# Decoder layer on one core: another split of the row-maximum pieces between the first stage and the attention loop

## The reference, cut to what matters

```
scores = jnp.einsum('bhqd,bhkd->bhqk', q, k) / jnp.sqrt(jnp.float32(Dh))
causal = jnp.tril(jnp.ones((S, S), dtype=bool))
scores = jnp.where(causal[None, None], scores, jnp.float32(-jnp.inf))
attn = jax.nn.softmax(scores, axis=-1)
out = jnp.einsum('bhqk,bhkd->bhqd', attn, v)
```

## Time and profile before

| | |
|---|---|
| median of 3 runs | 839.01 us |
| profiled execution, its own time | 840.59 us |
| its span, first to last instruction | 838.9 us |
| granted TensorE clock, mean | 0.984 |
| first stage, up to the first scores | 0 to 87.99 us |
| attention, heads 0 to 15 | 87.99 to about 470.3 us |
| one head of the steady state | 23.75 us |
| PE busy in such a head | 23.40 us |
| DVE busy in such a head | 22.41 us |
| ACT busy in such a head | 19.00 us |

### The profile page before, as it was taken

One profiled execution on the slowest core, in us unless ns is written; L12 is line 12 of the kernel. 1 busy time (PEld: TensorE's weight loads), 2 busy tenths in 40 slices (PEclk: granted clock), 3 DMA queues, 4 the chain that ended last, 5 costly groups with the idle time before them and its releaser, 6 DMA issues. The chain is left out here.

```text
span 838.9 us, 19596 instructions
## 1 busy us (share of the span) xinstructions
PE 783.6 (93%) x7434; PEld 496.9 (59%) x7435; DVE 559.2 (67%) x1072; ACT 512.3 (61%) x756; POOL 303.8 (36%) x226
## 2 busy tenths in 40 slices
PE   5899899999999999999998797889999999999994
PEld 1367344444443444444433585778888888877883
DVE  4575699999999999999980496973333333222395
ACT  4441687778887877788879487254444444343543
POOL 5040595555333355554550112132333333301121
PEclk9999799999999999999999999999999999999998
DMA  8783343334444443334232598452222222221362
GB/s 295 131 214 152 113 152 108 103 123 133 143 151 152 152 132 109 105 133 139 106 115 114 209 398 214 150 190 65 77 75 75 75 75 75 76 58 52 102 195 76
DMA packets 68362, 111.47 MB, mean 133 GB/s; under 512 B 39485, under 2 KB 49918, under 8 KB 63934
## 3 DMA queue, kind: packets, MB, share of 16 engines
q1 hardware_dynamic: 63134, 93.36, 35.7%
q0 software_dynamic: 4816, 16.65, 6.0%
q10 hardware_dynamic: 336, 0.40, 0.4%
HBM read 66.60 MB, written 32.37 MB: 118 GB/s over the span
## 5 line engine op out<-in xcount | busy, mean ns | idle before, releaser
L172 DVE TENSOR_REDUCE partial<-ring 128x1 f32<-128x512 f32 (+3 forms) x510 | 312.8, 670 | 24.2 <-PE ring L154 18.8
L709 ACT ACTIVATE probs<-scores 128x1024 f32<-128x1024 f32 (+1 forms) x320 | 270.5, 902 | 69.6 <-PE scores L747 36.9
L1284 ACT ACTIVATE hid<-turned 128x512 f32<-128x512 f32 (+1 forms) x112 | 65.6, 586 | 160.7 <-PE turned L1445 130.9
L154 PE MATMUL ring<-kstack,qstack 48*128 48x512 f16 (+1 forms) x581 | 156.4, 354 | 2.4 <-DVE partial L172 0.2
L774 PE MATMUL acc<-probs,values 128*32 128x512 f32 (+2 forms) x1472 | 156.6, 496 | 0.5 <-ACT acc_sb L714 0.3
L1470 PE MATMUL ops<-weights,work 128*128 (+1 forms) x1320 | 148.9, 273 | 2.7 <-DVE work L1685 1.4
L1445 PE MATMUL turned<-mats,weights 128*128 128x256 f16 (+1 forms) x1344 | 143.6, 262 | 3.2 <-DMA mats<-attn 2.2
L747 PE MATMUL scores<-qstack,kstack 49*128 49x512 f16 (+3 forms) x640 | 135.1, 352 | 7.2 <-ACT probs L709 5.9
L1685 DVE TENSOR_TENSOR work<-hid,work 128x512 f16<-128x512 f32 (+1 forms) x112 | 76.8, 690 | 94.9 <-ACT work L1289 94.8
L1470 PEld LDWEIGHTS ops<-weights,work 128*128 128x128 f16 x1320 | 128.4, 98 | 18.9 <-issue 3.8
L684 POOL TENSOR_TENSOR a_w_in<-a_w_in,w_scale 128x2304 f32<-128x2304 f32 x16 | 64.4, 4027 | 202.6 <-DMA a_w_in<-w_all 202.6
(11 more groups left out here) (203 smaller groups left out, 742.5 us busy)
## 6 DMA issues: line engine op xcount, KB each, us to landing
a_w_in<-w_all SPq DMA_DIRECT2D x16, 1152.0 KB, 9.1
w_split_d<-a_w_out SPq DMA_DIRECT2D x16, 1152.0 KB, 5.7
weights<-w_split_d SPq DMA_DIRECT2D x6, 2048.0 KB, 19.8
weights<-w_split_d POOLq DMA_DIRECT2D x3, 2048.0 KB, 12.1
qstack<-q_split SPq DMA_DIRECT2D x72, 64.0 KB, 2.7
kstack<-k_split SPq DMA_DIRECT2D x72, 64.0 KB, 2.8
weights<-by_token SPq DMA_DIRECT2D x8, 512.0 KB, 7.6
attn<-xT SPq DMA_DIRECT2D x4, 512.0 KB, 7.4
```

The source lines that it names most:

```text
L154: mm = nc.tensor.matmul(bank[:, at:at + w], qstack[rows, slot, t * P:(t + 1) * P], kstack[rows, slot, c:c + w], start=True, stop=not diagonal)
L172: return nc.vector.tensor_reduce(out=found[:, places[0]:places[-1] + 1:step], in_=bank[:, 0:WIDTH[n]].rearrange("p (k w) -> p k w", k=len( ...
L709: nc.scalar.activation(probs[:, quad % NPROBS, at:at + w], scores[half][:, first:first + w], ACT.Exp, scale=QK_SCALE).then_inc(exp_done, 1)
L1284: nc.scalar.activation(h32, hps[b].rearrange("p (j n) -> p j n", n=TW)[:, :, 0:w], ACT.Silu, scale=1.0 / WSCALE).then_inc(silu_done, 1)
```

## The change

It changes how many pieces stand where. No matmul and no reduction is added or dropped over the whole kernel.

- The first stage forms all 35 pieces of head 0 and all of head 1 (70 in place of 50). `pieces_behind` puts a pair behind every t step and behind every second m step but the last.
- The 490 pieces that are left, of heads 2 to 15, form one sequence, each head's in the order of the string `ORDER`. `deal_ring` fills the places of heads 0 to 14 with it: 34 in each of heads 0 to 2, 33 in each of heads 3 to 13, 25 in head 14.
- The places of a head hold 33 pieces: quad 1 has one in place of two behind its weighing, and quad 8 loses the one behind its first half. Kinds are no longer tied to quads; a head's q piece drifts from quad 1 (head 0) to quad 9 (head 13).
- The turned maximum M of a head stands wherever 4 pieces have passed since its last piece. It drifts with the sequence: M1 at the very start, M3 in quad 2 of head 2, M7 in quad 4 of head 6, M13 in quad 8 of head 12. M14 stands behind the weighing of quad 8 of head 13. M15 stands at quad 8 of head 14, right after the last piece.
- PE waits for a stack at the first piece of each head. `neg_max` of head 1 is reduced at the start of `attend`.

```
-EARLY_QUADS = tuple(range(6, NQUAD))
+ORDER = "wdwwnwqwdnwwwwpwdwwwnwwwwdwwwwwpwnw"
-PLACES = (("", "wd", "w"), ("w", "w", "nw"), ("", "ww", "w"), ("d", "w", "w"), ("", "ww", "Fwp"),
+PLACES = (("", "xx", "x"), ("x", "x", "x"), ("", "xx", "x"), ("x", "x", "x"), ("", "xx", "Fxx"),
...
+FIRST_HEADS = 2
+BEHIND = 4
...
+def deal_ring():
+    left = [("piece", g, n) for g in range(FIRST_HEADS, H) for n in ORDERED]
+    rows = [(g, 0) for g in range(1, FIRST_HEADS)]
...
+                if rows and (passed >= rows[0][1] + BEHIND or not left or rows[0][1] == 0):
+                    entries.append(("max", rows.pop(0)[0], 0))
+                for x in place + ("x" if (s, i) == (1, 2) and h < more else ""):
+                    if x in OTHERS and h > 0:
+                        entries.append((OTHERS[x], h - 1, 0))
+                    if x == "x" and left:
+                        entries.append(left.pop(0))
+                        passed += 1
+                        if not left or left[0][1] != entries[-1][1]:
+                            rows.append((entries[-1][1], passed))
...
-FIRST_PIECES = [*range(NPIECE), *EARLY_PIECES]
+FIRST_PIECES = FIRST_HEADS * [*range(NPIECE)]
...
     if kind == "m":
-        return 2 if n % 4 == 3 else 0
-    return 2 * {"qk": n >= NQ * 4 - 2, "v": n % 2, "t": n % 3 != 2}[kind]
+        return 2 if n % 2 == 1 and n < DC * CT - 1 else 0
+    return 2 * {"qk": n >= NQ * 4 - 2, "v": n % 2, "t": 1}[kind]
...
+                        if e == FIRST_PIECE[g]:
+                            pe.wait_ge(stack_in[g % NSTACK], (g // NSTACK + 1) * STACK_DMAS)
...
+            find_max(1)
```

More of the change, by code:

```diff
@@ L108, in deal_pieces @@
         left.setdefault(kind_of(n), []).append(n)
-    dealt = [[[x if x in OTHERS else left[x].pop(0) for x in place] for place in places] for places in PLACES]
-    assert not any(left.values())
-    return dealt
-DEALT = deal_pieces()
-EARLY_PIECES = [x for s in EARLY_QUADS for place in DEALT[s] for x in place if x not in OTHERS]
-def ring_of(h):
-    def entry(s, x):
-        kind, ahead = OTHERS[x] if x in OTHERS else ("piece", 2 if s in EARLY_QUADS else 1)
-        return (kind, h + ahead, 0 if x in OTHERS else x)
-    return [[[y for y in (entry(s, x) for x in place) if 0 <= y[1] < H] for place in places] for s, places in enumerate(DEALT)]
-RING = [ring_of(h) for h in range(H)]
+    return [left[x].pop(0) for x in ORDER]
+ORDERED = order_pieces()
+def deal_ring():
+    left = [("piece", g, n) for g in range(FIRST_HEADS, H) for n in ORDERED]
+    rows = [(g, 0) for g in range(1, FIRST_HEADS)]
+    more = len(left) - (H - 1) * len("".join(x for places in PLACES for place in places for x in place if x == "x"))
+    more += sum(x == "x" for places in PLACES[NQUAD - 2:] for place in places for x in place)
+    dealt, passed = [], 0
+    for h in range(H):
+        dealt.append([])
+        for s, places in enumerate(PLACES):
+            dealt[h].append([])
+            for i, place in enumerate(places):
+                entries = []
+                if rows and (passed >= rows[0][1] + BEHIND or not left or rows[0][1] == 0):
[8 more added lines that the diff above has]
+                            rows.append((entries[-1][1], passed))
+                dealt[h][s].append(entries)
+    assert not left and not rows
+    return dealt
+RING = deal_ring()
 RING_END = [("fold", H - 1, 0), ("turn", H - 1, 0)]
@@ L132 @@
 FOLDS = [sum(x[0] == "fold" for x in ENTRIES[0:e + 1]) for e in range(len(ENTRIES))]
-LAST_PIECE = {g: e for e, (kind, g, _) in enumerate(ENTRIES) if kind == "piece"}
+FIRST_PIECE, LAST_PIECE = {}, {}
+for e, (kind, g, _) in enumerate(ENTRIES):
+    if kind == "piece":
+        FIRST_PIECE.setdefault(g, e)
+        LAST_PIECE[g] = e
 VFIRST = NT - 5
-FIRST_PIECES = [*range(NPIECE), *EARLY_PIECES]
+FIRST_PIECES = FIRST_HEADS * [*range(NPIECE)]
 def group_rows(group, rows):
@@ L816, in _ @@
                 for s in range(NQUAD):
-                    ahead = h + (2 if s in EARLY_QUADS else 1)
-                    if ahead < H and s in (0, EARLY_QUADS[0]):
-                        pe.wait_ge(stack_in[ahead % NSTACK], (ahead // NSTACK + 1) * STACK_DMAS)
                     for half in range(2):
```

13 lines of the change are left out of this document (7 added, 6 removed).

## The result

The kernel after takes 847.38 us, the median of 4 runs (846.15 to 849.92), where the kernel before took 838.94 beside it (4 runs, 837.18 to 839.31). The ratio is 1.0109, 95% interval 1.0081 to 1.0136: slower by 1.1%, where 836.1 us and a range up to 841.5 were forecast. The profiled execution took 846.15 us, with a span of 844.4.

The account below looks back on a forecast made before the run. PE bounds the first stage; in the loop ACT and PE pace part A (quads 2 to 6), PE and DVE part B (quads 7 to 9, 0, 1). 5.5 - 10.2 + 1.8 = -2.9 us, so 836.1 us, range 831 to 841.5.

Parts of the forecast that it names:

- First stage, +5.5: End of the first stage: ten added pairs at 0.51 us of PE, plus 0.4 for hiding matmuls, cost 5.5 us.
- Rival 3: First stage: DVE falls behind, so the ten pairs cost about 8.5 us, not 5.5; 839 us; chance 0.12.
- End of the loop, +1.8: Head 14 and loop end: fuller quads 6 and 7 0.3, M15's wait 1.1, M14's later row 0.4; 1.8 us.
- rival 4: Seam into the loop: different work spacing spares PE's slow 1.2 GHz stretch, winning 3 us; 833 us; chance 0.12.
- Heads 1 to 13, -9.9 forecast: Attention loop: heads 1 to 5 win 1.05 us each, 6 to 9 0.6, 10 to 13 0.55.
- Quad 8 loses the q piece: Quad 8 and part B: removing q, M and two late bank waits gives 1.27 us, 1.1 after M's new cost.
- In quads 2 to 4 PE has waits for ACT to hide it: Attention loop: q's extra 0.45 us over a w piece is hidden in quads 2 to 4, not in 5 and 6.
- M costs 0.12 to 0.25 where it goes: Attention loop: the moved turned maximum costs 0.12 to 0.25 us in its new quad.
- The second piece behind quad 1: nothing is won there: Quad 1: the removed piece ran beside the first on PE, winning nothing; DVE saves 0.61 us part A doesn't need.
- Rival 2: Loop's PE queue: work only moves, a head wins 0.3 us; 842.1 us; decides below 0.52 a head; chance 0.20.
- Rival 1: Attention loop: DVE alone paces the heads, each piece less worth 0.614 us in all 14 heads; 830.9 us; chance 0.10.
- The prediction's own sign of being wrong: Wrong if heads' gain doesn't depend on where q stands, or the first stage's end moves over 7 us.

Follow-up runs that it names:

- Half reductions: Kernels before and after, each reduction reading only half its columns, so part of the maximum is left out: 828.35 and 838.09 us, one run each.
- after_again: The kernel after, unchanged, profiled and timed once more: 847.10 us, ratio 1.0090 to the kernel before.
- q_fixed: Kernel after with each head's q piece put back into the first half of quad 8: 844.40 us, ratio 1.0054 to the kernel before.
- row_by_place: Kernel before with the turned maximum M moved to seven other places, one in each of seven heads; all is computed: 839.85 us, one run.
- q_and_row_fixed: Kernel after with both q and the turned maximum M back in the first half of quad 8: 841.98 us, ratio 1.0032 to the kernel before.
- item 8: Kernel before with q of eight heads exchanged for a w piece of another quad; all is computed: 846.81 us, one run.
- item 9: The run row_by_place: kernel before with M in seven other places, 839.85 us.
- item 3: The half-reduction runs of the kernels before and after: 828.35 and 838.09 us, one run each.
- two_left_out: Kernel before without two w pieces a head, of quads 8 and 9, in heads 0 to 13; part of the maximum left out: 833.87 us, one run.

## Why the prediction was wrong

**First stage, +5.5: right.** 5.49 us by the two traces, 1.38 us for four products and a pair, no hold-up on DVE. Half reductions make the stretch 0.3 us shorter in both kernels (32.35 and 37.82 us) and leave 5.47 between them, so DVE has no part in it. Rival 3 is out.

**End of the loop, +1.8: right in kind, a little large.** +1.3 in all. The wait for M15's maximum is 0.91 us and makes its quad 1.1 longer (forecast 1.1), but the next interval gives 0.45 back. M14's row costs 0.4 at the start of head 14 (3.00 us for interval 0, forecast 0.4), but only 0.15 in after_again and nothing in q_fixed, with M14 in the same place, so that this hit is in part luck. Quads 6 and 7, with six pieces more, cost 0.2 (forecast 0.3).

**The seam, rival 4: it happened in the profiles, beside the rest.** Head 0 won 2.4 us, where 0.3 was forecast, by a shorter stretch at 1.2 GHz. But row_by_place, whose code is that of the kernel before up to there, shows 3.4 us too and a head 0 of 22.13 us. So this is no gain of the change: at an equal slow stretch head 0 wins nothing.

**Heads 1 to 13, -9.9 forecast, +1.75 measured: this step failed**, by 11.7 us. The medians missed the forecast by 11.3 (the profiled executions by 8.4, since the profile of after was lucky by 2.1 at the seam and by 1.2 ahead of the loop, 1.0 of it before the first t step). Without this luck the parts are 5.5 + 0 + 1.75 + 1.3, some 8.6 us of loss, near the 8.4 of the medians. The forecast gave a head 0.76 us on average and it lost 0.13, a gap of 0.9. With q and M back in quad 8 (q_and_row_fixed) a head takes 23.59: 0.3 of the gap is their drift, and the other 0.6 is that two pieces fewer are worth 0.16 us there. In the table, interval 8 gives 0.63 and the nine others together take 0.76. By the terms of the prediction:

- "Quad 8 loses the q piece, 0.67 us of PE, and M, 0.25; two late banks 0.35." Interval 8 did fall, by 0.63. But a q there was worth no more than a w (item 8), M was worth 0.20 (item 9), and nothing was won where the late banks are, though shorter reductions win 0.41 there (item 3): intervals 9 and 0 together went from 4.96 to 5.11. Quads 8 and 9 still carry four pieces each, nearly all of them 512 columns wide now. I had priced q by PE's time in a place where ACT and DVE are as full as PE. The busy columns of part B are sums over five quads, 12.01 us long, and hid that ACT, idle for 3.4 us of it, is busy in every moment of interval 8.
- "In quads 2 to 4 PE has waits for ACT to hide it." There is one such wait in a head, of 0.19 us, and the profile of the kernel before shows no other wait of PE in heads 1 to 13; it can't hide 0.45. In intervals 3 and 4 PE is busy all the time (2.04 of 2.04 us and 2.11 of 2.11). q costs 0.36, 0.22 and 0.43 in these quads.
- "M costs 0.12 to 0.25 where it goes": it costs 0.5 in quad 7, 0.3 net of what quad 8 wins.
- "The second piece behind quad 1: nothing is won there." Right, and it should have rung a bell. Of the two places that the change removes, one is worth nothing; the other, in quad 8, gives 0.63 with M, and q and M cost about that where they go. A w behind quad 9 would have been worth 0.42.

The kernel after shows all of it in one stretch. PE in interval 5 of head 6, 3.46 us where 3.06 stood before:

```profile
245.60 0.28 PE L833 MATMUL ring<-ident,neg_max 128*16 128x128 f32 x1
245.81 1.07 PE L806 MATMUL ring<-acc_sb,fold 128*32 128x512 f32 x8
246.80 0.39 PE L178 MATMUL ring<-kstack,qstack 48*128 48x512 f16 x2
...
246.96 0.22 PE L178 MATMUL ring<-kstack,qstack 48*128 48x128 f16 x1
...
247.25 0.22 PE L178 MATMUL ring<-kstack,qstack 48*128 48x128 f16 x1
```

M, the fold, a w and q stand in a row, and the scores that ACT waits for come behind them at 247.26. ACT waits 0.40 us for them:

```profile
247.93 1.30 ACT L733 ACTIVATE probs<-scores 128x640 f32<-128x640 f32 x2 [0.40 <-PE scores L780]
```

DVE waits behind a fold too, in head 5 for 0.98 us, in place of 0.57 in the earlier trace rows:

```profile
223.88 4.37 DVE L196 TENSOR_REDUCE partial<-ring 128x1 f32<-128x512 f32 x7 [0.98 <-PE ring L178]
```

Rival 2 (work only moves) is what happened, and it was still too kind: it gave a head 0.3 us, where it lost 0.13. Its point of decision, 0.52 us a head, held. Rival 1 is out: two pieces fewer won nothing, and half of DVE's work in reductions gone won 0.8 us of a head and not more. The prediction's own sign of being wrong is there: heads 1 to 5 take 23.85 us on average, 6 to 9 23.96, 10 to 13 23.86, which differ by 0.11 at most, where a step of 0.45 was forecast.

What stays open: which engine sets interval 8; why a piece behind quads 6 and 7 costs 0.5 to 0.6 and behind quad 8 0.25, beyond that DVE is full in the first case; how the rest of M's price divides; and in interval 0, how much of a late piece is the landing of the row. In two_left_out that interval is 2.15 us in seven heads of 1 to 13 and 2.40 to 2.56 in six, with nothing changed between them. The prices of a w were taken with 33 pieces in a head and those of q and M with 35, so a schedule that changes several at once may pay others.

## What to carry to other kernels

Where three engines hand each other work through a short ring, a piece of work has no price of its own but one for each place, for a plain piece here between nothing and the whole 0.6 us that a reduction takes; find it by one run that puts it somewhere else in each round of the loop, before building a schedule on it. Read the busy columns per step and not over half a round: what is taken from an engine in a step where another is full becomes waiting. A full column names a candidate and no more: interval 2 stayed at 2.25 us when PE or DVE had less to do, but interval 8 got shorter when DVE had less, with ACT full before and after. A run that relieves one engine tells more. And when a change frees work, look first at which places it frees and where the special items go that no longer have a fixed place.

## What was not expected of the hardware

The same code showed slow stretches of TensorE's clock of different length. At the loop's start PE ran at 1.2 GHz for 10.2 us in six of the nine profiles with 50 pieces in the first stage and for 3.4 us in the other three, and for 3.4 or 6.8 us in all nine with 64 or 70. Between the profiles of before and row_by_place, with the same code up to there, 6.8 us less of it made head 0 2.67 us shorter. The 3.4 us near 33 us are missing in three of the eighteen profiles, that of after among them; the first t step starts at 52.29 to 52.88 us in these three and at 53.40 to 55.38 in the others. Two profiles are to be compared by their clocks before their spans are.
